# The passage from the last attention heads to the FFN, rearranged, with small moves at the start, in the early heads and at the end

## The reference, cut to what matters

```python
# layer 0, attention: 16 heads of 128 over (2, 512, 256)
x = (h - mean(h)) * rsqrt(var(h) + eps) * ln_g + ln_b
q, k, v = rope(x @ wq.T + bq), rope(x @ wk.T + bk), x @ wv.T + bv
attn = softmax(where(causal, -inf, q @ k.T / sqrt(128)))
h = (attn @ v) @ wo.T + bo + residual
# layer 0, FFN: hidden 2048, 4-bit codes with a scale for every 32
Wg, Wu, Wd = (LUT16[nibbles(packed)] * scale for each of gate, up, down)
out = (gelu(x @ Wg.T) * (x @ Wu.T)) @ Wd.T
# layer 1, linear attention, 16 heads of 16, and layer 1, FFN: hidden 688, weights lut[idx]
```

## Time and profile before

| what | us |
|---|---|
| median of 3 executions | 596.62 |
| lowest, highest | 596.55, 596.65 |
| profiled execution | 598.54 |
| its span, first to last instruction | 596.2 |
| TensorE busy in the span | 537.3 |
| DVE, ScalarE, POOL busy | 475.5, 387.0, 389.3 |
| granted TensorE clock, mean | 0.985 |

### The profile page before, as it was taken

How to read it: one execution, slowest core, us unless ns; L and a number is a source line. 1 busy time by engine, 2 the same in 40 slices (tenths; PEclk the granted TensorE clock), 3 DMA queues, 4 the chain that set the end, 5 groups by cost and what they waited for, 6 DMA issues and landing times.

```text
span 596.2 us, 11417 instructions
## 1 busy us (share of the span) xinstructions
PE 537.3 (90%) x4186; PEld 363.3 (61%) x4186; DVE 475.5 (80%) x931; ACT 387.0 (65%) x843; POOL 389.3 (65%) x335
## 2 busy tenths in 40 slices
PE   7569899989899999999998688998999999999894
PEld 3246666656566665666655444554689778756672
DVE  6779999989899888899997776776637796767655
ACT  3487679687777887757889556556676556556230
POOL 1877979899998899978875487852132464434432
PEclk9789999999999999999999999999999999999997
DMA  8234635536374253582533432321200000000002
GB/s 292 71 81 109 131 77 133 86 90 149 60 146 85 58 81 72 117 168 54 89 59 76 115 106 75 111 64 50 71 22 16 2 1 1 1 1 1 1 2 70
DMA packets 98407, 44.62 MB, mean 75 GB/s; under 512 B 88240, under 2 KB 90672, under 8 KB 98352
## 3 DMA queue, kind: packets, MB, share of 16 engines
q1 hardware_dynamic: 97360, 43.35, 32.2%
q10 hardware_dynamic: 992, 0.55, 0.3%
HBM read 21.86 MB, written 1.05 MB: 38 GB/s over the span
## 4 chain that ended last, share of the span: by engine, by line
PE 46%; DVE 19%; issue 10%; POOL 9%; ACT 7%; DMA 1%; SPq 1%; POOLq 0%; DVEq 0%; ACTq 0%
PE bank L1515 40%; PE bank L1687 4%; DVE parts L1117 3%; POOL rr L560 2%; POOL qkl L564 2%; DVE vl L1125 2%; DVE nmax L1095 2%; POOL rr L533 2%; DMA pT<-parts 1%; DVE turned L1104 1%; ACT bank L731 1%; POOL rr L534 1%; ACT vh L755 1%; DVE turned L1106 1%; DVE w_all_l L1045 1%
## 5 line engine op out<-in xcount | busy, mean ns | idle before, releaser
L1515 PE MATMUL bank<-xTh,w_all_h 128*128 128x512 f16 (+2 forms) x392 | 130.6, 333 | 7.8 <-DVE w_all_l L1045 4.3
L1515 PE MATMUL bank<-xTh,w_all_l 128*128 128x512 f16 (+2 forms) x392 | 130.3, 332 | 0.0
L1515 PE MATMUL bank<-xTl,w_all_h 128*128 128x512 f16 (+2 forms) x392 | 130.3, 332 | 0.0
L564 POOL TENSOR_TENSOR qkl<-turned,qkh 128x512 f16<-128x512 f32 (+1 forms) x44 | 53.3, 1211 | 91.9 <-ACT qkh L844 91.6
L533 POOL TENSOR_TENSOR rr<-turned 64x512 f32<-64x512 f32 x64 | 94.6, 1477 | 28.0 <-DVE turned L1106 24.6
L731 ACT ACTIVATE bank<-bank,nmax 128x128 f32<-128x128 f32 (+3 forms) x128 | 64.1, 501 | 47.8 <-DVE nmax L1095 47.1
L541 POOL TENSOR_TENSOR qkl<-rr,qkh 128x512 f16<-128x512 f32 x64 | 73.9, 1159 | 22.9 <-ACT qkh L750 20.4
L534 POOL TENSOR_TENSOR rr<-turned 64x512 f32<-64x512 f32 x64 | 82.8, 1293 | 3.7
L844 ACT ACTIVATE qkh<-turned 128x512 f16<-128x512 f32 (+1 forms) x44 | 27.7, 629 | 60.3 <-DVE turned L1295 60.3
L1117 DVE SCALAR_TENSOR_TENSOR parts<-bank,rscaled,parts 128x128 f16<-128x128 f32 (+3 forms) x128 | 65.2, 546 | 0.1
L1095 DVE TENSOR_REDUCE nmax<-bank 128x1 f32<-128x128 f32 (+3 forms) x128 | 57.7, 483 | 6.9 <-PE bank L1559 5.8
(11 more groups left out here) (201 smaller groups left out, 1480.2 us busy)
## 6 DMA issues: line engine op xcount, KB each, us to landing
stage<-in_per_head SPq DMA_DIRECT2D x16, 512.0 KB, 4.1
xa<-in_codes SPq DMA_DIRECT2D x32, 128.0 KB, 2.8
stage<-in_packed SPq DMA_DIRECT2D x12, 256.0 KB, 2.8
stage<-in_scales SPq DMA_DIRECT2D x12, 256.0 KB, 3.4
pT<-parts SPq DMA_TRANSPOSE x128, 2.8
x<-in_x SPq DMA_DIRECT2D x2, 512.0 KB, 6.9
stage<-in_w1T SPq DMA_DIRECT2D x2, 512.0 KB, 3.9
rope<-in_ropes ACTq DMA_DIRECT2D x1, 512.0 KB, 9.2
```

The costliest lines, as they stand in the source:

```text
L564: pool.tensor_tensor(il[n % 2][0:rows, :], inter[0:rows, n % 2, :], ih[n % 2][0:rows, :], ALU.subtract).then_inc(g_il, 1)
L1515: last = pe.matmul(dst, l, r, start=start and i == 0, stop=stop and i == 2, skip_group_check=skip)
```

## The change

It does five things. The second batch's x, 512 KB in one transfer, becomes four of 128 KB, each with a semaphore that the statistics wait for one by one. The low halves of the weights of heads 6 and 8 move from the ends of steps 3 and 6 to those of steps 4 and 7. The bias is added by POOL one row tile a step, in steps 8 to 15. In the passage, pairs 0 and 1 of the fields get memory of their own (`xa`'s first half and `hot_more`), w32 gets a third buffer, pair 0 is unpacked at the end of step 29 and pair 1 within step 30 between the maxima and `inverse`; POOL scales four pieces before run 1 instead of three; both halves of batch 0's turning go through one bank, one in step 31 and one in step 32; the gate product of piece 0 is issued in step 32 before weigh(31), the up product in step 33 before out_project(31); in run 1 the tables `SCALED_AT` and `HIGH_AT` take the place of `unpack_beside`, and DVE takes the low half one m after ScalarE the high one. ScalarE's `spread_entry` copies move from steps 27 to 31 to m = 4, 6, 8, 11; SP loads pieces 4 and 5 before the transposes of unit 31; the turning of batch 1 is one product earlier on TensorE (k = 25 for 26) and its high half at m = 12 for 13. The last `down` does the products with ih first and waits for il only before those that read it. Left out of the diff are renamings and arguments passed on.

```diff
 GROUP = 6
-LATE_LOWS = (3, 5, 6, 8, 10, 11, 13, 14, 16, 18, 20, 21)
+LATE_LOWS = (4, 5, 7, 8, 10, 11, 13, 14, 16, 18, 20, 21)
...
 FIRST, OTHER = 1, 0
-RESIDUAL_STEPS = {9: 0, 12: 1}
+RESIDUAL_STEPS = (8, 9, 10, 11, 12, 13, 14, 15)
...
 X0_NORM_AT = {0: (OTHER, "nrm"), 6: (FIRST, "xa"), 11: (OTHER, "xa")}
-BYTES_AT = (27, 28, 29, 31)
+BYTES_AT = (25, 27, 28, 29)
...
 Q_PIECES = 3 * MLP // Q_COLS
-UNPACK_AT = {1: 2, 4: 3, 6: 4, 9: 5}
+UNPACK_AT = {2: 3, 4: 4, 7: 5}
+SCALED_AT = {0: 4, 1: 5, 3: 6, 4: 7, 5: 8, 6: 9, 8: 10, 9: 11}
+HIGH_AT = {0: 3, 1: 4, 2: 5, 4: 6, 5: 7, 6: 8, 7: 9, 9: 10, 10: 11}
+ENTRIES_AT = {4: 0, 6: 2, 8: 4, 11: 6}
...
         side_bank = bank[6:8]
-        w32 = [rr, rope]
-        bits = [prob[:, 0, 2 * i:2 * i + 2, :].rearrange("p e n -> p (e n)").bitcast(U8).rearrange(
-            "p (e i n) -> p e i n", i=2, n=Q_COLS) for i in range(2)]
+        w32 = [rope, rr, turned[:, 1, 2:4, :]]
+        bits = [a.rearrange("p e n -> p (e n)").bitcast(U8).rearrange("p (e i n) -> p e i n", i=2, n=Q_COLS)
+                for a in (xa[:, 0:TPB, :], hot_more[:, :, :, :].rearrange("p e i n -> p e (i n)"), prob[:, 0, 0:2, :], prob[:, 0, 2:4, :])]
...
+        def bits_of(pair):
...
+            return bits[pair if pair < 2 else 2 + pair % 2]
...
         s_x = [sem("s_x0"), sem("s_x1")]
+        s_first = [sem(f"s_first{t}") for t in range(TPB)]
...
         def turn_bank(phase, b, c):
-            return (proj_bank, S_bank[0])[c] if (phase, b) == (1, 0) else side_bank[c]
+            return proj_bank if (phase, b) == (1, 0) else side_bank[c]
...
-            load_x(FIRST)
+            for t in range(TPB):
+                row = FIRST * TPB + t
+                sp.dma_start(x[:, row, :], x_tok[:, row, :]).then_inc(s_first[t], 16)
...
             for s in STEPS:
+                if s == UNITS - 1:
+                    load_fp4(4)
+                    load_fp4(5)
...
                         load_fp4(j)
-            for j in range(4, Q_PIECES):
+            for j in range(6, Q_PIECES):
...
             sp.wait_ge(d_acc, B)
+            sp.wait_ge(g_w32, 2 * NIBBLES)
...
+            def residual(i):
...
+                b = (FIRST, OTHER)[i // TPB]
+                t = b * TPB + i % TPB
...
                 pool.wait_ge(a_xa, place(b) + 1)
...
+                pool.wait_ge(d_part, 1)
+                pool.tensor_tensor(xa[:, t, :], xa[:, t, :], bo_row[:, :], ALU.add).then_inc(g_res, 1)
...
                 if s in RESIDUAL_STEPS:
-                    residual((FIRST, OTHER)[RESIDUAL_STEPS[s]])
+                    residual(RESIDUAL_STEPS.index(s))
...
-                if j >= 2:
-                    pool.wait_ge(d_fl, j - 1)
+                if j >= 3:
+                    pool.wait_ge(d_fl, j - 2)
...
+                    pool.tensor_tensor(w32[j % 3][:, c, :], code, scl[:, j % 4, :], ALU.mult).then_inc(g_w32, 1)
...
-            for j in range(3):
+            for j in range(4):
...
                 low_inter(m)
-                if m == 1:
+                if m == 2:
...
+                if m in SCALED_AT:
+                    scaled(SCALED_AT[m])
...
-            def high_xT(phase, b):
-                for c in range(KC):
+                act.activation(fh[w][:, :, cols], w32[j % 3][:, :, :], ACT.Copy, scale=W_SCALE * FP4_AS_FP8).then_inc(a_fh, 1)
...
+            def high_xT(phase, b, cs=range(KC)):
+                for c in cs:
...
-            def gated(n, func, rows=P, between=lambda: None):
+            def gate_of(n, func, rows=P):
...
                                scale=1 / (X_SCALE * W_SCALE)).then_inc(a_gelu, 1)
+            def gated(n, func, rows=P, between=lambda: None):
...
+                if n:
+                    gate_of(n, func, rows)
...
             for s in STEPS:
+                if s == UNITS + 1:
+                    gate_of(0, ACT.Gelu_apprx_tanh)
...
                     to_bytes(BYTES_AT.index(s))
-                    for e in range(2):
-                        spread_entry(2 * BYTES_AT.index(s) + e)
-                if s == UNITS:
+                if s == UNITS - 1:
+                    high_xT(1, 0, (0,))
...
                     high_fp4(0)
-                    high_xT(1, 0)
-            act.wait_ge(t_v, UNITS)
-            high_fp4(1)
+                if s == UNITS:
+                    high_xT(1, 0, (1,))
+                    act.wait_ge(t_v, UNITS)
+                    high_fp4(1)
+                    high_fp4(2)
...
                 if m == 0:
-                    high_fp4(2)
+                    to_bytes(4)
+                    to_bytes(5)
...
                 gated(m, ACT.Gelu_apprx_tanh, P, lambda: between_first(m))
-                if m and unpack_beside(m - 1):
-                    high_fp4(unpack_beside(m - 1))
+                if m in HIGH_AT:
+                    high_fp4(HIGH_AT[m])
+                if m in ENTRIES_AT:
+                    for e in range(2):
+                        spread_entry(ENTRIES_AT[m] + e)
...
                     weights_of_pair(LOOKED_UP_AT[m])
-                if m == 13:
+                if m == 12:
...
                 for t in ts:
+                    if b == FIRST:
+                        dve.wait_ge(s_first[t], 16)
...
                     top(s, 3)
+                if s == UNITS - 2:
+                    unpacked(1)
+                    signed(1)
...
                 step(s)
-                if s == UNITS - 1:
-                    dve.wait_ge(t_pv, UNITS - 1)
+                if s == UNITS - 3:
...
                     signed(0)
+                if s == UNITS - 1:
+                    low_xT(1, 0, (0,))
+                    low_fp4(0)
...
                 if s == UNITS:
-                    low_fp4(0)
-                    low_xT(1, 0)
-            low_fp4(1)
-            unpacked(1)
-            signed(1)
+                    low_xT(1, 0, (1,))
+                    low_fp4(1)
+                    low_fp4(2)
+            product_of(0)
...
             attention_sums(1)
+            dve.wait_ge(t_pv, UNITS - 1)
+            unpacked(2)
+            signed(2)
...
             for m in range(M_TILES):
-                product_of(m)
-                if m == 0:
-                    low_fp4(2)
+                if m:
+                    product_of(m)
...
                     signed(UNPACK_AT[m])
-                if m and unpack_beside(m - 1):
-                    low_fp4(unpack_beside(m - 1))
+                if m - 1 in HIGH_AT:
+                    low_fp4(HIGH_AT[m - 1])
...
+                if s == UNITS - 1:
+                    pe.wait_ge(d_rope, 2 * UNITS)
+                    turn_norm(1, 0, even_odd, (0,))
+                if s == UNITS:
+                    pe.wait_ge(d_xTl, TURNS.index((1, 0)) * KC + 1)
+                    turn_norm(1, 0, even_odd, (1,))
+                if s == UNITS + 1:
+                    gate_up(0, fp4_weights(0), whole, beside_first, 0, (1,))
...
                     out_project(s - 2)
+                if s == UNITS:
+                    pe.wait_ge(d_pl, TPB * UNITS)
+                    pe.wait_ge(d_xTl, (TURNS.index((1, 0)) + 1) * KC)
+                    gate_up(0, fp4_weights(0), whole, beside_first, 0, (0,))
...
                     project(s + 2, 1)
-                if s == UNITS:
-                    pe.wait_ge(d_rope, 2 * UNITS)
-                    pe.wait_ge(d_pl, TPB * UNITS)
-                    turn_norm(1, 0, even_odd)
...
+            def gate_up(n, weights, rows, beside, k, ws=(0, 1)):
...
+            def last_down(n, weights):
...
+                tiles, _, row_tiles = pieces_of(n)
+                for hidden, terms, ready in ((ih, (0, 1), a_ih), (il, (0,), g_il)):
+                    pe.wait_ge(ready, n + 1)
+                    for i, m in enumerate(tiles):
+                        ws = weights(2, m, 0)
+                        for j, t in enumerate(row_tiles):
+                            o = i * UNIT + j * P
+                            for term in terms:
+                                last = pe.matmul(acc_bank[t // 2 % 2][:, t % 2 * D:t % 2 * D + D], hidden[n % 2][0:i_rows(m), o:o + P],
+                                                 ws[term], start=False, stop=False, skip_group_check=True)
+                last.then_inc(t_down, 1)
...
             def beside_first(k):
-                if k == 26:
+                if k == 25:
...
-            pe.wait_ge(d_ol, UNITS)
-            pe.wait_ge(d_xTl, (TURNS.index((1, 0)) + 1) * KC)
-            all_rows = lambda m: P
...
             for m in range(M_TILES):
-                gate_up(RUN1 + m, fp4_weights(0), all_rows, beside_first, 2 * m)
+                if m:
+                    gate_up(RUN1 + m, fp4_weights(0), whole, beside_first, 2 * m)
...
-            down(RUN4 + I_TILES - 1, table_weights(1), i_rows)
+            last_down(RUN4 + I_TILES - 1, table_weights(1))
```

48 lines of the change are left out of this document (19 added, 29 removed).

## The result

The changed kernel takes 592.3 us (median of 4 executions, 591.5 to 593.5); the kernel before took 596.6 beside it. The ratio is 0.9933, 95% interval 0.9916 to 0.9951. Forecast were 591.2 and a range of 586.5 to 596.3.

The account below looks back on a forecast made before the run. TensorE, busy 537.3 of 596.2 us, was taken as the bound, so only its standing counts. Terms of -0.1, -0.1, -0.4, +4.1, -3.6, -2.5, -1.5 and -1.3 sum to -5.4 from the median 596.62: 591.2, range 586.5 to 596.3.

Parts of the forecast that it names:

- Unpacking: Pairs 0 and 1 beside heads 30 and 31: head 31's scores +4.1 us; +1.4 unhindered, +9.0 if every operation is held.
- The rival of unhindered work: Unpacking beside POOL's rotations is not held: +1.4 us instead of +4.1, total 588.5; chance 0.24.
- one sign against it: Against unhindered unpacking: the six cases of unpacking line L1081, running from 0.28 to 1.25 us.
- Heads: Low halves of heads 6 and 8 moved: -0.10 us together, with head 4 at 9.05, head 5 9.22, head 8 10.54.
- the residual: One POOL add after each of steps 8 to 15: 2.94 us to win, +2.54 lost to holds, net -0.40.
- Passage: From head 31's scores into the first down products: down(0) at T + 20.15, -3.6 us, from -2.6 to -4.3.
- Run 1: From down(0) to down(11): DVE's wait for ScalarE goes, POOL's load stays; -2.5 us, from 0 to -5.
- Turn: Second half's turning moved earlier, removing TensorE's wait before its look-up: -1.5 us, from 0 to -1.6.
- Last down: Eight of the last down's 12 matmuls need only ih, ready one subtraction earlier: -1.3 us, from -0.9 to -1.6.
- Start: x in four transfers, so statistics begin under the transfer: -0.1 us, from -0.3 to +0.3.
- run 1 keeping its waits: Rival: POOL's 4.5 us a piece stays the bound, 593.7, or the early heads lose, 595; chance 0.17.
- the slower case: Rival: both unpackings held at each operation, +9.0 us, and no gain from down(0) to down(11): 598.6; chance 0.09.

Follow-up runs that it names:

- Run 6: Changed kernel with pair 1 unpacked behind head 30's low halves of the probabilities and POOL's first scaling waiting for it: 590.41 us.
- run 2: Changed kernel with the third late low half back at step 6 instead of step 7: 589.96 us.
- Run 5: Changed kernel with only ScalarE's queue changed: table entries at m = 4, 10, 11, 13 and byte conversions ahead of the FP4 high halves: 591.72 us.
- run 12: Changed kernel with x's first half in one transfer, third late low half at step 6, paired residual adds, later pair 1 unpacking, bytes before FP4 halves: 583.64 us.
- run 9: Changed kernel with the turn of the second half and the split of the last down product undone: 594.33 us.
- run 10: The changed kernel itself measured again, with no edit: 592.52 us.
- run 3: Changed kernel with pairs 0 and 1 unpacked one step earlier each, ahead of DVE's second rotation: 591.38 us.
- run 8: Changed kernel with sixteen products of zeros in TensorE's wait ahead of head 1's projection: 596.03 us.

## Why the prediction was right, and where its steps were not

**Unpacking, right, the largest term.** +4.1 forecast, +3.45 measured, and the signs named for it are there: three operations at 1.36 to 1.41 beside POOL. The turn taking was a little kinder than counted: of the five operations two went together (314.04 and 314.39) and three were held, so `inverse` came 8.4 us behind head 30's scores (318.61 - 310.22) and not 9.0 (321.5 - 312.50). Run 6 shows the mechanism by taking away the meeting: 1.97 went for good. The rival of unhindered work did not come, though one sign against it was read too strongly: of L1081's six cases in the kernel before, two are long (1.19 and 1.25) and four are 0.28 to 0.29.

**Heads, right in kind, the residual too dear.** Head 4 at 9.04, head 5 at 9.21 and head 8 at 10.54 are the forecast numbers, and run 2 shows that step 6 to 7 cost 1.49. Of the residual the places were right (heads 9, 11, 12, 14, 15) and the hold was not: they are 9.50 against 9.22 for a head that begins with a low half alone, a hold of 0.28 where 0.44 was counted. Five times the 0.16 make -1.20 out of -0.40.

**Passage, right in kind, 0.95 short.** down(0) stands 21.12 behind head 31's scores, forecast 20.15. Forecast with every matmul at the high clock, it ran partly at the low one, 0.88 over 322 to 335. In run 2, whose row for that window has 1.00, it is 20.47. So 0.65 goes with the clock, and 0.3 stays open. Whether TensorE's standing in head 30 brought the low clock is not shown: run 2 has the same standing and a row of 1.00 for the window behind it. The gain itself is read at the stage alone, since no run takes the new order of the passage back.

**Run 1 is the step that failed.** -2.5 forecast, -1.43 measured; the standing before down(2) to down(11) went from 6.04 to 4.67, not below 3.5. The wait at DVE's low halves did go, has no counterpart. But the forecast charged the rest to POOL's load, at half a microsecond for each full m, and gave ScalarE's small copies "some", without a figure. In its place came ScalarE's queue ahead of the gelu:

```profile
369.01 1.06 ACT L813 ACTIVATE w_all_h<-turned 128x1024 f16<-128x1024 f32 x1 [1.77 <-POOL turned L569]
...
370.93 1.13 ACT L802 ACTIVATE xT<-stage 128x512 uint8<-128x512 int32 x2
371.97 0.57 ACT L847 ACTIVATE turned<-bank 128x512 f32<-128x512 f32 x1
```

Piece 8, four table copies and two conversions stand before gelu 7, and DVE's product waited 4.55 for it. Runs 5 and 12 show that as the cause of the wait before down(7), and run 12 that it is the order: the conversions stood behind piece 8, for which ScalarE idled 1.77. Run 5 shows the table entries as half of the wait before down(8). The third, 1.28 before down(6), stayed in every run that kept POOL's order. In the trace of the kernel after, two scalings of POOL take 4.12 in place of 2.16, beside two low halves of DVE; that this is its cause is argued only.

```profile
364.86 4.12 POOL L569 TENSOR_TENSOR turned<-pT,stage 128x512 f32<-128x512 fp8e4 x2
```

**Turn, right.** -1.5 forecast; by run 9 it is worth 1.64. The other 0.52 of the stage's -2.16 is won in run 9 too, where the look-up's bracket is 1.02 against 1.53 before, so it belongs to other edits. **Last down, right by luck.** -1.3 against -1.39, of which run 9 finds 0.87 in the edit; the rest belonged to the low clock on the twelve products, which the term had taken as given.

**Start, wrong and small.** -0.1 (at most +0.3) forecast; the split costs 0.7 at head 0's scores, beyond the bound. What the forecast had left out is that the first weights and the other half's x are issued later by the three extra issues and land later. The -0.61 in the table is that cost and a gain by the clock, which comes and goes with the same code (run 10).

**The total.** 592.3 lies 1.1 above the forecast, though the traces show 6.4 for a forecast of 5.4. Two profiled executions differ by chance by up to 3.3 us at head 2 alone, and head 24 is 9.5 to 10.6 long (in the two longest TensorE waits for its transposes); so medians of four carry, by an estimate from the runs' spreads, about a microsecond either way. That the sum came so near is luck in part, too: unpacking, residual, start and turn came out 0.5 to 0.8 better each, passage and run 1 each 1.0 to 1.1 worse. The rivals: run 1 keeping its waits came half true, and unhindered unpacking and the slower case did not come.

## What to carry to other kernels

Before work is moved beside another engine's, look at what that engine does in the same microseconds and at what stands behind the work on its own: the same unpacking cost 3.4 us (changed kernel), 3.7 (run 3) and 1.5 (run 6) from head 28 on, and the cheapest place needed one more wait, on the engine with slack. When a wait is removed from one queue, list the whole of the queue that now arrives last, the small copies too, since an order that frees one wait can put the next one there. Compare traces by stage, from mark to mark, and let the medians judge only sums of several microseconds.

## What the runs showed of the hardware that was not expected

The low clock in the first 40 us falls in different places with the same code, for 44.68 to 48.00 us at head 2's scores, and filling one idle stretch moved it and made the median 3.7 us slower (run 8). Holding goes both ways: POOL's two scalings took 4.12 in place of 2.16 beside DVE's low halves, while those took 2.17 and 1.52 where they take 1.22 alone. And the turns do not fall one by one: of five operations of DVE beside POOL's, the second went straight behind the first (314.04 and 314.39) and POOL's took 1.41 in place of 1.26, while the last three waited for one of POOL's each. What decides that is not shown.
